# A graph kernel in which SyncE fetches three tiles of every 128 instead of one of every 96

## The reference, cut to what matters

```python
def _rgcn_layer(x, W, root, bias, src, dst, seg):          # 8 relations, 6250 nodes, D = 256
    agg = segment_sum(x[src], seg, num_segments=8 * 6250)  # 206250 edges
    agg = agg.reshape(8, 6250, -1)
    return einsum('rnd,rde->ne', agg, W) + x @ root + bias

xn = layernorm(x)
h = relu(_rgcn_layer(xn, W[0], ...)); h = relu(_rgcn_layer(h, W[1], ...))
h = sigmoid(_rgcn_layer(h, W[2], ...))
x = x + h + mix(xn)          # linear attention with 8 heads, then a two-layer perceptron
x = x + moe(layernorm(x))    # 8 experts, the best 2 of each token
```

## Time and profile before

| | |
|---|---|
| median of 3 runs | 6456.33 us (6443.06 to 6458.41) |
| the profiled execution | 6445.27 us, span 6443.5 us from its first to its last instruction |
| layer 1, first to last gather on POOL | from 376 to 2371 us |
| layer 2 | from 2390 to 4394 us |
| layer 3 | from 4413 to 6412 us |
| gathers on POOL | 4788 |
| rows fetched by SP | 6144 |

### The profile page before, as it was taken

The page is one execution under the profiler, slowest core; times in us unless marked ns, Lnnn a source line. Parts: engine busy times, 40 slices in busy tenths (PEclk is TensorE's granted clock), DMA queues, the critical chain, the costliest instruction groups (busy, mean ns, idle before and its releaser), DMA issues.

```text
span 6443.5 us, 106263 instructions
## 1 busy us (share of the span) xinstructions
PE 5449.1 (85%) x22890; PEld 3937.1 (61%) x22890; DVE 2213.7 (34%) x6194; ACT 1048.4 (16%) x2707; POOL 4590.0 (71%) x4872
## 2 busy tenths in 40 slices
PE   8977777777777778888888888888888888888888
PEld 3445555555555546666666666665777777777777
DVE  8931212221122223333333333333444444444444
ACT  2211111111111111111111111111222222222222
POOL 1157777777777767777777777776777777777776
PEclk9989998999998989999999999999999999999999
DMA  6654444444444445555555555555444444444443
GB/s 203 185 154 140 140 140 140 139 140 140 140 141 140 140 145 154 149 150 149 149 150 149 150 147 149 152 149 152 118 117 118 118 118 118 119 118 118 118 117 96
DMA packets 371700, 896.30 MB, mean 139 GB/s; under 512 B 92490, under 2 KB 197902, under 8 KB 352695
## 3 DMA queue, kind: packets, MB, share of 16 engines
q0 software_dynamic: 229776, 627.62, 33.6%
q10 hardware_dynamic: 114178, 243.16, 12.7%
q1 hardware_dynamic: 27116, 18.64, 1.0%
HBM read 697.14 MB, written 185.61 MB: 137 GB/s over the span
## 4 chain that ended last, share of the span: by engine, by line
POOL 59%; issue 19%; PE 13%; DMA 5%; DVE 3%; POOLq 1%; SPq 1%; ACT 0%; DVEq 0%; ACTq 0%
POOL ring L611 59%; DMA ring<-table,gather_idx 4%; PE ps_out L1532 4%; PE ps_y L1503 3%; DVE hT L1075 1%; PE ps_y L1797 1%; PE ps_c L1503 1%; PE ps_b L1503 1%; PE ps_tr L1712 1%; PE ps_b L1808 0%; POOLq L602 0%; PE ps_c L1700 0%; PE ps_c L1667 0%; PE ps_c L1808 0%; SPq L474 0%
## 5 line engine op out<-in xcount | busy, mean ns | idle before, releaser
L611 POOL DMA_INDIRECT ring<-table,gather_idx x4788 | 4541.4, 948 | 1506.5 <-issue 1482.2
L1532 PE MATMUL ps_out<-ring,onehot 128*125 x8400 | 2333.3, 422 | 776.5 <-SPq L510 718.1
L1532 PEld LDWEIGHTS ps_out<-ring,onehot 128*125 128x125 f32 x8400 | 1629.5, 206 | 1347.5 <-issue 1129.0
L1503 PE MATMUL ps_y<-W,hT 128*125 128x512 f32 (+1 forms) x2400 | 1011.5, 562 | 17.3 <-DVE hT L1075 11.5
L946 DVE COPY y_stage<-ps_y 125x512 f32<-125x512 f32 x150 | 103.6, 691 | 2220.9 <-PE ps_y L1503 2218.6
L1532 PE MATMUL ps_out<-ring,onehot_more 128*125 x2448 | 659.7, 414 | 116.0 <-SPq L510 61.9
L1503 PEld LDWEIGHTS ps_y<-W,hT 128*125 128x125 f32 x2400 | 453.2, 190 | 429.1 <-issue 403.5
L1119 DVE TENSOR_TENSOR onehot<-targets,ps_out 128x500 f32<-128x500 f32 x1050 | 646.4, 671 | 172.4 <-issue 118.1
L1532 PEld LDWEIGHTS ps_out<-ring,onehot_more 128*125 128x125 f32 x2448 | 459.5, 199 | 290.4 <-issue 229.8
L627 ACT COPY y_stage<-ps_y 125x512 f32<-125x512 f32 x350 | 204.8, 585 | 1825.5 <-PE ps_y L1503 1783.7
L1119 DVE TENSOR_TENSOR onehot_more<-targets,ps_out 128x250 f32<-128x250 f32 x612 | 241.3, 414 | 580.8 <-PE ps_out L1532 462.7
(11 more groups left out here) (194 smaller groups left out, 3352.3 us busy)
## 6 DMA issues: line engine op xcount, KB each, us to landing
table<-y_stage ACTq DMA_DIRECT2D x147, 896.0 KB
own_tile<-table SPq DMA_DIRECT2D x6144, 1.0 KB
ring<-table,gather_idx POOLq DMA_INDIRECT x4788
table<-y_stage ACTq DMA_DIRECT2D x147, 104.0 KB
xn_in<-xn_scratch ACTq DMA_DIRECT2D x100, 125.0 KB
base<-y_stage ACTq DMA_DIRECT2D x100, 125.0 KB
base_in<-base ACTq DMA_DIRECT2D x100, 125.0 KB
x_in<-in_x_dram ACTq DMA_DIRECT2D x75, 125.0 KB
```

Source lines behind the costliest of these rows:

```text
L611: nc.gpsimd.indirect_dma_start(ring[0:n, c * D:(c + 1) * D], None, table[l], bass.IndirectOffsetOnAxis(ap=gather_idx[0:n, tile:tile + 1].b ...
L1503: last = nc.tensor.matmul(BANK[phase][b][0:WIN, 0:n], hT[parity][:, k, :], W[:, k, b * 2 * D:b * 2 * D + n], start=(k == 0), stop=(k == K ...
L1532: return nc.tensor.matmul(ps_out[w % 2][0:WIN, 0:D], lhsT, ring[:, bass.ds(slot + j * D, D)], start=first, stop=last)
```

## The change

SP fetches the last three tiles of a group, and a group is 32 chunks (`TURNS` 4 instead of 3). A layer has 12 groups, again 384 chunks. POOL leaves out 36 tiles of a layer in place of 16. A group has 384 rows, of which SP issues seven behind each of the first 54 halves and six behind the 55th; the copy into the ring, now of 384 KB, stands behind the 60th half, and the wait for it ahead of the last two halves (the first of which has one tile of each kind).

The row numbers are multiplied by 1024 once, in the preparation, by the ScalarE instruction that turned them into integers. So a loaded register is itself the byte offset, the line of register arithmetic is left out, and one load brings 16 offsets. The table is seen as one long row of bytes. The numbers of a group lie on 12 partitions of 32 in `rows_now`, one DMA of 1.5 KB.

```diff
-TURNS = 3
-ROWS_A_HALF = 3
+TURNS = 4
+OWN_TILES = 3
+ROWS_A_HALF = 7
+ROWS_A_LOAD = 16
+ROWS_A_LINE = 32
...
-            four = [sp.alloc_register(f"row{i}") for i in range(4)]
+            at_byte = [sp.alloc_register(f"at_byte{i}") for i in range(ROWS_A_LOAD)]
+            table_bytes = [a.rearrange("(o n) d -> o (n d)", o=1).bitcast(U8) for a in table]

             def fetch_row(l, r):
-                if r % 4 == 0:
-                    sp.load(four, rows_now[0:1, r:r + 4])
-                row = sp.snap(four[r % 4], min_val=0, max_val=nodes * R - 1)
-                sp.dma_start(own_tile[r:r + 1, :], table[l][bass.ds(row, 1), :]).then_inc(rows_landed, 16)
+                j, p = r // TILE, r % TILE
+                line, at = r // ROWS_A_LINE, r % ROWS_A_LINE
+                if at % ROWS_A_LOAD == 0:
+                    sp.load(at_byte, rows_now[line:line + 1, at:at + ROWS_A_LOAD])
+                byte = bass.RuntimeValue.of_register_unchecked(at_byte[r % ROWS_A_LOAD]
+                                                               ).with_bounds(min_val=0, max_val=(nodes * R - 1) * ROW_BYTES)
+                sp.dma_start(own_tiles[p:p + 1, j * D:(j + 1) * D].bitcast(U8),
+                             table_bytes[l][:, bass.ds(byte, ROW_BYTES)]).then_inc(rows_landed, 16)

             def own_to_ring(chunk):
-                sp.wait_ge(rows_landed, 16 * TILE)
+                sp.wait_ge(rows_landed, 16 * OWN_ROWS)
                 sp.sem_clear(rows_landed)
                 sp.wait_ge(slots_free, chunk + 1)
-                c = (OWN % RING) * TILES + TILES - 1
-                sp.dma_start(ring[:, c * D:(c + 1) * D], own_tile[:, :]).then_inc(own_landed, 16)
+                c = (OWN % RING + 1) * TILES
+                sp.dma_start(ring[:, (c - OWN_TILES) * D:c * D], own_tiles[:, :]).then_inc(own_landed, 16)
...
                         for j in range(TILES):
-                            if chunk < GROUPS * GROUP and chunk % GROUP == OWN and j == TILES - 1:
+                            if chunk < GROUPS * GROUP and chunk % GROUP == OWN and j >= TILES - OWN_TILES:
                                 continue
...
-                    nc.scalar.copy(prep_t[:, :], prep_f[:, :]).then_inc(rows_whole, 1)
+                    nc.scalar.activation(prep_t[:, :], prep_f[:, :], ACT.Copy, scale=float(ROW_BYTES)).then_inc(rows_whole, 1)
```

More of the change, by code:

```diff
@@ L22 @@
 U32 = mybir.dt.uint32
+U8 = mybir.dt.uint8
 ACT = mybir.ActivationFunctionType
@@ L69, in gps_program @@
     OWN = GROUP - 1
-    FETCHES = -(-TILE // ROWS_A_HALF)
+    OWN_ROWS = OWN_TILES * TILE
+    FETCHES = -(-OWN_ROWS // ROWS_A_HALF)
     COPY_AT = 2 * GROUP - 4
-    assert FETCHES <= COPY_AT - 1
+    assert FETCHES <= COPY_AT - 1 and 1 <= OWN_TILES <= TILES and TURNS > 1
+    OWN_IN_HALF = [max(0, min(HALF, OWN_TILES - TILES + (h + 1) * HALF)) for h in range(TILES // HALF)]
+    ROW_BYTES = 4 * D
+    assert nodes * R * ROW_BYTES < 1 << 31 and ROW_BYTES & (ROW_BYTES - 1) == 0
     QK = 4 * KR
@@ L80, in gps_program @@
     res_dram = nc.dram_tensor("res_scratch", [nodes, D], FP32).ap()
[L81 removed]
+    own_rows = nc.dram_tensor("own_rows", [GROUPS, OWN_ROWS], I32).ap()
     with ExitStack() as ctx:
@@ L104, in gps_program @@
         ring = sb("ring", [128, RING * TILES * D])
-        own_tile = sb("own_tile", [128, D])
-        rows_now = sb("rows_now", [1, TILE], I32)
+        own_tiles = sb("own_tiles", [TILE, OWN_TILES * D])
+        rows_now = sb("rows_now", [OWN_ROWS // ROWS_A_LINE, ROWS_A_LINE], I32)
         onehot = [sb(f"onehot{i}", [128, TILES, WIN]) for i in range(STATIC)]
@@ L459, in _ @@
             for g in range(GROUPS):
-                tile = (g * GROUP + OWN) * TILES + TILES - 1
+                tile = (g * GROUP + OWN + 1) * TILES - OWN_TILES
                 b, p = tile // 128, tile % 128
-                sp.dma_start(own_rows[g:g + 1, :], prep_t[p:p + 1, b * 128:(b + 1) * 128]).then_inc(rows_kept, 16)
+                sp.dma_start(own_rows[g:g + 1, :].rearrange("o (j r) -> (o j) r", j=OWN_TILES),
+                             prep_t[p:p + OWN_TILES, b * 128:(b + 1) * 128]).then_inc(rows_kept, 16)
             sp.wait_ge(rows_kept, 16 * GROUPS)
@@ L490, in _ @@
                     chunks = sp.snap(round_ * CHUNKS)
-                    before_fewer = sp.snap(round_ * ((BODIES - 1) * 16 * HALF - 16 * GROUPS) + 16 * HALF)
+                    before_fewer = [sp.snap(round_ * ((BODIES - 1) * 16 * HALF - 16 * own * GROUPS) + 16 * HALF)
+                                    for own in OWN_IN_HALF]
                     with sp.Fori(0, GROUPS) as group:
-                        sp.dma_start(rows_now[:, :], own_rows[bass.ds(group, 1), :]).then_inc(rows_read, 16)
+                        sp.dma_start(rows_now[:, :], own_rows[bass.ds(group, 1), :].rearrange("o (j r) -> (o j) r", r=ROWS_A_LINE)
+                                     ).then_inc(rows_read, 16)
                         done = sp.snap((round_ * GROUPS + group) * 16 + 16)
@@ L499, in _ @@
                             own = turn == TURNS - 1
-                            fewer = sp.snap(group * (TURNS * 16 * HALF - 16) + before_fewer + (turn * 16 * HALF - 16 * own))
+                            fewer = [sp.snap(group * (TURNS * 16 * HALF - 16 * n) + b + (turn * 16 * HALF - 16 * n * own))
+                                     for n, b in zip(OWN_IN_HALF, before_fewer)]
                             for s in range(RING):
                                 for h in range(TILES // HALF):
-                                    if (s, h) == (OWN % RING, TILES // HALF - 1):
-                                        sp.wait_ge(gathered[s][h], fewer)
+                                    if s == OWN % RING and OWN_IN_HALF[h]:
+                                        sp.wait_ge(gathered[s][h], fewer[h])
                                         if own:
@@ L510, in _ @@
                                     sp.sem_inc(halves_ready, 1)
-                                    for r in range(at * ROWS_A_HALF, min((at + 1) * ROWS_A_HALF, TILE)):
+                                    for r in range(at * ROWS_A_HALF, min((at + 1) * ROWS_A_HALF, OWN_ROWS)):
                                         fetch_row(l, r)
@@ L517, in _ @@
                         landed = [sp.snap(turn * (16 * HALF) + n) for n in before]
-                        fewer = sp.snap(turn * (16 * HALF) + before_fewer - 16 * GROUPS)
+                        fewer = [sp.snap(turn * (16 * HALF) + b - 16 * n * GROUPS) for n, b in zip(OWN_IN_HALF, before_fewer)]
                         for s in range(RING):
                             for h in range(TILES // HALF):
-                                if (s, h) == (OWN % RING, TILES // HALF - 1):
-                                    sp.wait_ge(gathered[s][h], fewer)
+                                if s == OWN % RING and OWN_IN_HALF[h]:
+                                    sp.wait_ge(gathered[s][h], fewer[h])
                                 else:
```

## The result

The changed kernel takes 7317.96 us (median, 7309.7 to 7326.33), the kernel before 6456.23 on the same chip: 1.134 times as long, with a 95% interval of 1.1316 to 1.1363. That is 862 us more, where 54 more were forecast, and above the upper end of the range, 6640. The profiled execution took 7309.7 us, its span is 7307.9.

The account below looks back on a forecast made before the run. POOL's gathers, 1.253 us a tile, were taken as the bound. From 6445.3 us, layers 1 and 2 add 50 each and layer 3 saves 25: 6520, less 10 for partly hidden terms, 6510 us (1.0% slower); range 6370 to 6640.

Parts of the forecast that it names:

- The bound now: Inside the layers POOL's gathers set the pace, 1.253 us a tile, though TensorE is busier (85% against 71%).
- The row: SP's step from row to row falls from 0.418 to 0.334 us without register arithmetic; 384 rows take 128.3 us a group.
- The load: SP's load of sixteen registers takes 0.60 us like one of four (0.46 to 2.4); 24 take 14.4 us a group.
- a margin of 5: In layer 3 SP's group, 151.3 us, stays 5 us below POOL's 156.6.
- the dear load: Rival: sixteen registers take 2.4 us, total 7000 and more; at 1.0 us some 6800; within 0.14 for several slower cases.
- The turn: Between SP's groups, the branch and the reading of new row numbers take 4.3 us, as before.
- Stalls and copy: In layers 1 and 2, ScalarE's stores delay SP 7.8 us a group; late arrival at the ring copy costs 5.0 more.
- The cushion: The ring lets SP be some 25 us late before POOL waits; SP is 18 us late in the first group.
- The layers: Layers 1 and 2 each become 50 us longer, layer 3 25 us shorter.
- my own sign of a wrong forecast: The forecast is wrong if POOL's wait for TensorE stays under 40 us, or if layer 3 is slower too.
- the forecast's own rule: A layer's loss: 11 more groups times SP's excess over POOL (7.5 us), less 7 of cushion, less 25 of saved gathers.
- SP keeps pace: Rival: SP's group isn't over POOL's, or only slightly, so some or all of 75 us is gained: 6370 to 6425, chance 0.29.

Follow-up runs that it names:

- two of 128: Changed kernel with SP fetching two tiles of every 128 instead of three, five rows behind a half instead of seven: 6429.89 us, 0.9956 times the kernel before.
- one load a group: Changed kernel loading its sixteen registers once a group instead of 24 times, fetching the same 16 rows again: 6422.4 us, 0.9962 times the kernel before.
- nine of 160: Changed kernel with three tiles of every 160, nine groups a layer, six rows behind a half, 32 registers to a load: 6427.18 us, 0.9969 times before.
- fours: Changed kernel with four registers to a load instead of sixteen, 96 loads a group, all rows fetched: 8341.82 us in one execution.
- the fetch alone: Changed kernel's byte offsets and sixteen-register loads, but one tile of every 96 and three rows behind a half as before: 6459.15 us, 0.9999 times before.

## Why the prediction was wrong, point by point

**The bound now: right.** POOL set the pace at 1.253 us; after the change it took 1.254 between its waits, and two of 128 gained about that step for every gather left out. The question I called decisive, whether SP keeps 156.6 us, decided.

**The row: right.** From rows 6 I took 0.334 us. SP's timeline in layer 3, seven rows behind a half without a load:

```profile
5604.34 2.20 SPq L487 DMA_DIRECT2D own_tiles<-table  x7
```

(2.20 - 0.225) / 6 = 0.329. Taking the sum of the remaining instructions and their gaps was enough; the move stays with each row, as the trace of before had it.

**The load: the step that failed.** I wrote that one register took 0.462 and the shortest four 0.457, "so the number doesn't show", and carried 0.60 from four to sixteen. The two rows were true: both are one step. The inference was not: two sizes that cost the same say nothing of a size beyond them. I had the upper bound right (2.4) and the measured 1.24 + 0.04 lies under it; but a term that goes from 14 to 58 us a group against a margin of 5 was the widest of the whole sum, and I let it stand at its lower end and gave the dear load a part of the 0.14 for all that is slower. That rival's "1.0 us, some 6800" had the mechanism, and 1.24 goes on from there. The Trainium skill's rule ("Runtime: NRT & Kernel Launch", section "Instruction fetch mechanics"), which I set aside, gave 3.2 us and 62 more a group; the measured 1.24 is far under it, and it was right that the number shows.

**The turn: right in kind, too small.** 4.3 us were taken from before; measured are 5.9 to 8.1. The branch back and the wait for the row numbers both grew. The branch by line, for two turns (first and last start):

```profile
L507 SPq COMPARE_BRANCH  x2: 50/54/59, 2880.1 to 3073.8; - x2
L507 SPq FUSED_REGOPS  x2: 50/50/50, 2885.7 to 3076.5; - x2
```

From the branch to the next instruction 5.6 and 2.7 us pass, where the earlier trace rows have 2.6; the mean is 3.1, 4.3 and 3.5 us in the three layers, and was 2.6, 2.9 and 2.5 before. Single turns of up to 6.8 us make the difference. The longer loop body isn't it: with two registers to a load the body holds the most instructions of all kernels here, and the means are 2.6, 3.8 and 2.6.

**Stalls and copy: right in layers 1 and 2.** Rows with stalls 136.1 and 138.3 against 136.1; copy and last rows 5.7 and 4.9 against 5.0. In layer 3 I had no copy, since SP was to be in time; it was late there too, and paid 4.3. SP's waits over the span (us, times, longest), to be set beside the earlier trace rows:

```profile
SPq L527 <- DMA ring<-own_tiles: 114.5, 36, 8.1
SPq L526 <- DMA rows_now<-own_rows: 60.2, 27, 4.6
SPq L493 <- DMA own_tiles<-table: 47.2, 36, 4.4
```

Before, SP waited for 2 of 48 copies, now for 36 of 36, 3.2 us each: whoever comes late at a hand-over of its own pays for its latency as well.

**The cushion: right in kind.** I gave the ring 25 us and SP 18 us of lateness in the first group. POOL's first wait of over 2 us comes after gather 124 or 125 of a layer, at the end of its first group of 125, in all three layers. By the same reading as above, less the 1.8 us, SP is 33, 33 and 27 us late at its last rows in that group, where I had 18. Set beside the lateness of the half that lets TensorE free the slot, POOL's waits of over 1 us begin in layer 1 at 26 us (one load a group) and 28 (all loads), and nine of 160 has 27 without one, so the 25 was about right there. In layers 2 and 3 such waits stand from 13 to 22 us on; whether the ring holds less there or TensorE is itself behind isn't told apart.

**The layers: wrong.** Layer 3 was to be 25 us shorter and is 184 longer (2182 against 1998); it was my own sign of a wrong forecast. POOL's wait, forecast near 150 us and in layers 1 and 2 alone, is 934.6, with 210 of it in layer 3. Layers 1 and 2 were to lose 50 each and lost 306 and 353. By the forecast's own rule, with the measured groups, the layers lose 11 x (28.9 + 33.4 + 18.5) - 75 = 814 us before the cushion; 864 were measured. So the rule for turning groups into time was about right, some 50 us short, of which 18 lie behind the last gather.

**Was it the load alone?** Not quite. With the load at my 0.60 a group would still take 168, 172 and 159 us, from the turn, the copy in layer 3 and the register work. At the 35 us that the kernel gained for each us of a group between fours and sixteens, 17 us fewer make some 6700 (an estimate, and beyond the sizes that were run): still slower, and above my range. So of the 800 us between the forecast and the profiled execution about 600 are the load's and 200 the rest's. The run with one load shows the other end: even with loads at almost nothing the change gives 0.4%, not the 1.2% of the rival "SP keeps pace".

## What to carry to other kernels

When an engine that hands on another's work is given a task of its own, it has a budget: the other engine's pace times the work in a group. Write its stream out by instruction, and for any instruction whose size changes look for its price at three sizes, not two, before carrying it over; where the trace has none, let the wide term decide the forecast, not its cheap end. Fitting the budget on average isn't enough where the engine downstream has little slack: two of 128 with a quarter of SP's time to spare gained all that it promised, while groups that only just fitted lost part of it, or more, in layer 2.

## What the runs showed of the hardware that I had not expected

- SP's register load from SBUF costs about 0.24 us and 0.22 for each step (0.33 behind a transfer); a step brings four registers if the load begins at a multiple of 16 bytes and four are left, else one. This is fitted to loads of 1, 2, 4, 6, 8, 12, 16 and 32 registers. Four registers (0.559) are cheaper than two (0.734), and six cost 0.90 or 1.45 by their address.
- SP's branch back at the end of a group took some 2.6 us to the next instruction in most turns (2.6, 2.9 and 2.5 on average in the three layers before), but up to 6.8 in single ones of the changed kernel. In the fetch alone, with the shortest body, it took 0.27 us in layer 1 and 2.6 in layer 3. What decides wasn't tried; the length of the body alone doesn't.
- TensorE's 22890 instructions took 5866.6 us in place of 5449.1, while it stood waiting for SP longer; its granted clock goes between the two levels 1.2 and 2.4 GHz, and averaged 0.869 of the higher in place of 0.931. With two registers to a load the average was 0.706, and the kernel still grew by 36 us for each us of SP's group: SP's stream was the path, and the slower clock cost little here.
